# Gathering expert rows: waiting for the landing three places ahead instead of two

## The reference

```python
s = _L1_attn_ref(xn, wq, bq, wk, bk, wv, bv, wo, bo)        # 16 heads, softmax, per sequence
combine = combine.at[jnp.arange(T)[:, None], top_idx].set(top_w)   # eight weights per token
h1 = jax.nn.silu(jnp.einsum('th,eih->eti', x, w_gate))
routed = jnp.einsum('eti,ehi->th', h1 * combine.T[:, :, None], w_down)
g = silu(routed + shared)
x = x + s * g
```

## Time and profile before

| | us |
|---|---|
| median of three runs | 2050.67 (2048.13 to 2051.21) |
| the profiled execution, its own time | 2045.78 |
| its span | 2044.0 |

### The profile page before, as it was taken

The page is one execution under the profiler, slowest core; times in us unless marked ns, Lnnn a source line. Parts: engine busy times, 40 slices in busy tenths (PEclk is TensorE's granted clock), DMA queues, the critical chain, the costliest instruction groups (busy, mean ns, idle before and its releaser), DMA issues.

```text
span 2044.0 us, 49776 instructions
## 1 busy us (share of the span) xinstructions
PE 1820.5 (89%) x14389; PEld 1625.6 (80%) x14390; DVE 1273.6 (62%) x4624; ACT 887.8 (43%) x2899; POOL 625.9 (31%) x661
## 2 busy tenths in 40 slices
PE   4789999999999999377999999799999988888896
PEld 2467999999997778256999999688887877787785
DVE  4344445445444442888888888555554777677675
ACT  2212344444442221233666666444445555555453
POOL 0065000000005600005677776000000555555551
PEclk9889999999999995587999999899999899999996
DMA  9611011111101100301111111355555111111111
GB/s 375 251 41 44 18 36 36 38 38 36 36 26 41 44 0 0 131 32 39 47 50 50 52 51 47 144 172 174 167 171 160 44 40 39 39 40 40 39 40 52
DMA packets 153497, 149.29 MB, mean 73 GB/s; under 512 B 16931, under 2 KB 134374, under 8 KB 153062
## 3 DMA queue, kind: packets, MB, share of 16 engines
q1 hardware_dynamic: 130820, 100.98, 14.9%
q0 software_dynamic: 21760, 46.18, 7.7%
q10 hardware_dynamic: 866, 1.51, 0.2%
HBM read 70.95 MB, written 77.66 MB: 73 GB/s over the span
## 4 chain that ended last, share of the span: by engine, by line
PE 68%; DMA 12%; DVE 10%; issue 6%; ACT 3%; POOL 1%; DVEq 1%; ACTq 0%; POOLq 0%; SPq 0%
DMA rows_g<-ys_dram,slot 11%; PE ps_y L735 8%; PE ps_t L940 5%; PE ps_y L793 4%; PE ps_up L1050 4%; PE ps_up L784 4%; PE ps_t L1063 4%; PE ps_up L916 3%; PE ps_y L929 3%; PE ps_t L751 3%; PE ps_t L753 3%; PE ps_rec L750 3%; PE ps_rec L748 3%; PE ps_rec L1020 2%; PE ps_rec L884 2%
## 5 line engine op out<-in xcount | busy, mean ns | idle before, releaser
L479 POOL DMA_INDIRECT rows_g<-ys_dram,slot x256 | 242.6, 948 | 487.7 <-DMA ys_dram<-slots_y 306.4
L623 ACT ACTIVATE probs<-ps_up,negmax 128x256 f32<-128x256 f32 x512 | 240.7, 484 | 326.3 <-DVE negmax L1457 326.3
L469 POOL DMA_INDIRECT xs_dram<-xn_tok,slot x256 | 249.8, 976 | 314.0 <-DVE slot L1359 216.7
L940 PE MATMUL ps_t<-v_sb,probsT 128*128 128x64 f32 x2048 | 260.7, 271 | 2.0 <-DVE ctx_sb L1440 1.4
L940 PEld LDWEIGHTS ps_t<-v_sb,probsT 128*128 128x128 f32 x2048 | 252.1, 194 | 4.4 <-issue 4.3
L735 PE MATMUL ps_y<-zeros 128*128 128x512 bf16 x752 | 219.3, 381 | 0.0
L1216 DVE SCALAR_TENSOR_TENSOR mixn<-ps_rec,cols_sb,th_r 128x16 f32<-128x16 f32 x256 | 59.9, 234 | 244.0 <-PE ps_rec L750 142.1
L1457 DVE TENSOR_REDUCE negmax<-ps_up 128x2 f32<-128x512 f32 x256 | 164.8, 686 | 32.3 <-PE ps_up L916 31.8
L916 PE MATMUL ps_up<-kT,qT 64*128 64x256 f32 x1536 | 129.1, 301 | 61.4 <-DVE kT L1413 60.9
L916 PEld LDWEIGHTS ps_up<-kT,qT 64*128 64x128 f32 x1536 | 103.0, 191 | 82.2 <-issue 61.5
L929 PE MATMUL ps_y<-misc,probs 128*128 128x128 f32 x1024 | 163.6, 283 | 0.6 <-ACT probs L623 0.5
(11 more groups left out here) (241 smaller groups left out, 4457.6 us busy)
## 6 DMA issues: line engine op xcount, KB each, us to landing
xs_dram<-zeros SPq DMA_DIRECT2D x52, 512.0 KB, 5.9
slots_x<-xs_dram SPq DMA_DIRECT2D x88, 256.0 KB, 3.0
ys_dram<-slots_y SPq DMA_DIRECT2D x84, 256.0 KB, 2.5
slots_x<-xs_dram SPq DMA_DIRECT2D x41, 128.0 KB, 2.2
ys_dram<-slots_y SPq DMA_DIRECT2D x40, 128.0 KB, 1.8
gate<-w_gate SPq DMA_DIRECT2D x1, 5120.0 KB, 20.5
down<-w_down SPq DMA_DIRECT2D x1, 5120.0 KB, 15.2
w_sb<-w POOLq DMA_DIRECT2D x16, 256.0 KB, 4.8
```

Of the source, the lines that this page charges most:

```text
L469: nc.gpsimd.indirect_dma_start(xs_dram, bass.IndirectOffsetOnAxis(ap=slot[:, n, k:k + 1], axis=0), xn_tok[:, n, :], None).then_inc(scatter ...
L479: nc.gpsimd.indirect_dma_start(rows_g[:, i % 16, :], None, ys_dram, bass.IndirectOffsetOnAxis(ap=slot[:, i // TOPK1, i % TOPK1:i % TOPK1 + ...
L623: nc.scalar.activation(probs[:, a, i, :], ps_s[a][:, T * i:T * i + T], ACT.Exp, bias=negmax[:, a, i:i + 1], accum_out=sums[:, j % 4, i, a: ...
L940: last = nc.tensor.matmul(ps_ctx[:, P * i + HD * a:P * i + HD * a + HD], probsT[:, a, kc, P * i:P * i + P], v_sb[:, j % 2, kc, HD * a:HD * ...
```

## The change

Gather i waits for the landing of gather i - 3 instead of gather i - 2. Gather 2 has no such wait any more. The wait for a free place in the ring is as before.

```diff
             for i in range(NT * TOPK1):
                 if i >= 16:
                     pool.wait_ge(acc1_used, i - 15)
-                if i >= 2:
-                    pool.wait_ge(gathered[(i - 2) % 16], 16 * ((i - 2) // 16 + 1))
+                if i >= 3:
+                    pool.wait_ge(gathered[(i - 3) % 16], 16 * ((i - 3) // 16 + 1))
                 nc.gpsimd.indirect_dma_start(rows_g[:, i % 16, :], None, ys_dram,
```

## The result

The changed kernel takes 1979.57 us in the median (1975.46 to 1985.63, four runs), the kernel before 2049.4 us (2042.45 to 2051.21, four runs). The ratio is 0.9668 with a 95% interval of 0.9633 to 0.9702, some 68 us (the two medians lie 69.8 us apart). The forecast was 1992.5 us with a range of 1985 to 2004: right in its direction and its mechanism, wrong in its size.

A forecast was written before the change was run, and what follows sets the result against it. Gathers, two in flight, were taken to bound the second attention half. Savings of 57.4 us in 55 pairs and 0.8 us in the batch before, 58.2 us together, off 2050.67 us gave 1992.5 us, range 1985 to 2004 us.

The forecast's parts named there:

- The bound and the reading of the waits: Second attention half: gathers, two in flight, set the pace at 1.65 us a row, 6.6 us a pair; POOL's ring isn't full.
- Supply, 1.25 us a row: Second half's gathers become bound by POOL's issue after the change: 1.25 us a row, 5.0 us a pair.
- Demand, 5.58 us a pair: Second half's 55 pairs: DVE's chain takes 5.58 us a pair, PE's 5.51 us; saving 57.4 us.
- The batch before, 0.8 us: Batch ahead of the 55 pairs: only its last step is starved of rows, worth 0.8 us of saving.
- "The 37.85 us behind the last pair do not touch gathers": Part behind the second half's last pair: taken as unchanged by the change, no saving there.
- The base of the sum: Whole kernel: the 58.2 us saving was taken off the three runs' median, 2050.67 us; the profiled execution took 2045.78 us.
- Rival 1: Second half's gathers: landings stretch to 3.75 us with three in flight, pitch 1.5 us, saving 38 us, 2013 us; chance 0.05.
- rival 3: Second half's gathers: landings stretch to 5.0 us, 7.7 us a pair, 55 us more, 2106 us; chance 0.03.
- Rival 2: Second half's gathers: DVE's row sums block descriptor writing, third place buys nothing, within 4 us of 2051 us; chance 0.05.
- The port rule: Second half: by it DVE's two-input row sums would hold up gathers; the trace showed at most 0.16 us each.
- "Slower": Whole kernel: the sign of a longer time after the change, given only by rival 3; chance 0.03.

The follow-up runs named there:

- e2: Kernel before, still two places ahead, with the two wait lines exchanged (landing first, then free place): 1984.1 us against 2043.7 us.
- e18: The same exchange of the two wait lines in the kernel before, run once more in another set: 1980.7 us against 2044.8 us.
- e9: The kernel before, unchanged, run again with its own profile: 2044.5 us against 2045.8 us.
- e10: The changed kernel, run again beside the kernel before: 1979.3 us against 2045.8 us, ratio 0.9660.
- e16: Kernel before with two spare matmuls in each of PE's four waits behind the last pair: 2038.9 us against 2044.8 us.
- e17: Changed kernel with spare matmuls behind the last pair and at the start of the second half: 1977.3 us against 2044.8 us for the kernel before.
- e11: Changed kernel with two spare matmuls in each of PE's four waits behind the last pair: 1976.8 us against 2045.8 us for the kernel before.
- e3: Changed kernel, but two places ahead instead of three from gather 128 on: 1997.7 us against 2043.7 us for the kernel before.
- disturbed sets: Two of five follow-up sets, on one chip, where every kernel took 470 to 620 us longer; the changed kernel was 2.7% slower than the one before.

## Why the prediction was off

**The bound and the reading of the waits: right.** The gathers paced the half, and the 75.8 us of POOL for xn_tok were no full ring. In e2, still two places ahead but with the landing waited for in the gather, POOL's idle time before line 479 is put down to the landing for 77.0 us of the same stretch and to L1400 for 20.7 us.

**Supply, 1.25 us a row: right.** 1.25 us at the start, and depth four adds nothing. I took the 0.76 us between landing and next gather as given; some 0.5 us of it was the order of two wait lines (e2, e18).

**Demand, 5.58 us a pair: right.** 5.57 us between the copies shown, 310.3 us for the stretch against 310.5 us. The saving there was forecast as 57.4 us and is 57.6 us (56.7 us between e9 and e10).

**The batch before, 0.8 us: low by 1.0 to 2.7 us.** 46.43 us became 44.31 us, 2.1 us; between e9 and e10 it is 1.8 us, between e16 and e17 3.5 us. In the first two profiles the rest is the half's first pair, which took 6.75 us at the low clock before and 5.35 us after; such a first pair also came in e2 and e11. In e9 and e16 the first pair took 5.4 us, and there rows were late earlier in the batch: the profile that the forecast was read from hid part of the loss behind its slow first pair.

**"The 37.85 us behind the last pair do not touch gathers": the step that failed.** It was sized as 0 and measured 8.0 us between the first two profiles. The instructions there are the same, the clock is not. I had the low clock in front of me, 1.2 GHz in the earlier trace rows, and credited the stalls with it, but took the end at the clock it happened to show. What it is worth on average is less than 8.0 us. With the end at 29.7 to 29.8 us in both, e16 and e17 differ by 61.7 us, which is what the gathers' pace is worth, 3.5 us over the forecast's 58.2 us, most of it in the batch before. The filling gives the kernel before 5.9 us and the changed kernel 2.5 us with overlapping runs, so the change gains some 3 us at the end, an estimate from these medians. Why the unfilled changed kernel loses less there than the kernel before is argued, not shown. In profiles its clock held in one of four, in those of the kernel before (its own and e9) in none of two, too few to tell. Its gap ahead of L940 is 0.31 us and not 1.09 us, and where its clock fell, it fell later (7.9 us behind the last copy in e10, 3.7 and 3.6 us in the kernel before and in e9; ends of 34.7 to 36.0 us against 37.9 us). But e3, with late rows, has 1.26 us ahead of the same matmuls and an end of 29.7 us, so that gap is not the whole of it.

**The base of the sum: 4.9 us too high.** The saving was taken off 2050.67 us, the median of three executions, while the profiled one took 2045.78 us. In the undisturbed sets the kernel before took 2043.7 to 2045.8 us in the median of 9 to 21 executions. The 12.9 us between 1992.5 us and 1979.57 us are thus 4.9 us of base, 7.5 us between the forecast for the profiled execution (1987.6 us) and its 1980.08 us (8.0 us at the end, 1.3 us in the batch before, 0.2 us in the pairs, less the 2.0 us lost ahead of the half), and 0.5 us between that execution and the median.

**The rivals.** Rival 1 asked for landings of 3.75 us, rival 3 for over 4.26 us; the pitch of 1.25 us and the median landing of 2.5 us exclude both in the undisturbed sets. (Single late landings were there before the change too: the chain of waits of the kernel before has one of 3.90 us at 1653.08, over the 3.1 us that the prediction took as the longest.) Rival 2 asked for gathers held up by DVE: 0.944 us median and 1.064 us maximum beside a DVE that is busier than ever (269 us of 310 us). The port rule of the Trainium skill (SBUF — State Buffer, "Who interferes with whom"), as the prediction took it, is not borne out for these gathers beside L1400. The prediction joined two rules there that the page keeps apart: the same section says of tensor_tensor, as an inference, that it takes only the read side of the shared ports while writing descriptors needs the write side, and the box on blocked DMAs speaks of DVE's 2-port modes. The 0.944 us agree with that reading. "Slower" did occur, in the disturbed sets, with 7.5 us a pair where rival 3 had priced 7.7 us; that the numbers are close is chance, as the landings were not late and none of my rivals had that condition.

**The range** ended at 1985 us because its lower end held the end part fixed. Adding 0 to 8 us for a clock that my own rows showed at 0.50 would have put it at 1977 us; with the base of 2045.78 us alone it would have been 1980 us.

## What to carry to other kernels

Where DMAs are kept n in flight by a wait on the landing n places back, compute (landing + release) / n and compare it with the issue pitch and with what the consumer needs; the first n at which issue wins is enough. Look which of several waits sits in the DMA itself: putting the landing there was worth almost as much as a third place (55.6 and 54.7 us of the 57.6 us in the pairs). Take the saving off the same execution that it was read from. Treat PE's clock in short serial ends as a term with two values; here two spare matmuls per gap kept it at the high one in six profiles of six.

## What was not expected of the hardware

- A landing waited for ahead of a gather in its own instruction releases it after some 0.76 us (0.02 + 0.02 + 0.72 us in the chain of waits). Waited for in the gather itself, two gathers take 2.73 us instead of 3.27 us; with a landing of 2.5 us that leaves some 0.2 us, an estimate.
- POOL pauses once after gather 112 and once after 210 in the undisturbed kernels: 4.1 and 4.2 us from start to start in the kernel before, 2.9 and 3.2 us in the changed one, where the ring hides it. Without a lead it made the pairs of 8.99 and 8.95 us behind which the clock fell. The profile names no cause.
- The same program on the same chip ran 470 to 480 us longer for two whole sets of runs, and the sign of this change depended on it: 0.967 undisturbed, 1.027 disturbed. The attention nearly stood still there while POOL issued scatters.
